# Flamingo layer on one core: list ends cleared by one queue two experts ahead, the first batch's q, k and maxima in another order, the last norms moved up

## What is computed

```
x = x + tanh(g_xattn) * attention(layernorm(x), ctx, ctx)      # 16 heads of 16
    energy = einsum('nqhd,nkhd->nhqk', qh, kh); attn = softmax(energy / 4); out @ Wo.T + bo
x = x + tanh(g_ffn) * ffn(layernorm(x))
    scores = softmax(xf @ w_router); top 2 of 8 experts
    h = silu(xf @ w1) * (xf @ w3); y = h @ w2                   # hidden 512, for each expert
    out = shared / 3 + moe_out * 2 / 3
```

## Time and profile before

| | us |
|---|---|
| median of 3 runs | 816.92 (815.06 to 818.07) |
| the profiled execution | 814.12 |
| its span, first to last instruction | 812.4 |
| PE busy in the span | 769.9 (95%) |
| DVE, POOL, ACT busy | 538.8, 430.7, 413.4 |
| mean granted clock of PE | 0.992 of full |

### The profile page before, as it was taken

How to read it: one execution, slowest core, us unless ns; L and a number is a source line. 1 busy time by engine, 2 the same in 40 slices (tenths; PEclk the granted TensorE clock), 3 DMA queues, 4 the chain that set the end, 5 groups by cost and what they waited for, 6 DMA issues and landing times.

```text
span 812.4 us, 19406 instructions
## 1 busy us (share of the span) xinstructions
PE 769.9 (95%) x6955; PEld 686.5 (85%) x6956; DVE 538.8 (66%) x1118; ACT 413.4 (51%) x690; POOL 430.7 (53%) x489
## 2 busy tenths in 40 slices
PE   4888999999999998898997999999999999999998
PEld 3756777777777776578997999999999999999998
DVE  5677889998888888857644444444444444446897
ACT  5667777777777767653324333333334334333332
POOL 5633446666666654457772476656756675236000
PEclk9999999999999999999998999999999999999999
DMA  6854557776666654244394354444543422317622
GB/s 213 272 179 158 173 185 231 234 235 209 210 209 209 198 182 145 93 170 138 110 248 113 96 155 130 117 114 131 142 116 78 111 70 58 72 53 306 233 93 79
DMA packets 129150, 127.34 MB, mean 157 GB/s; under 512 B 55232, under 2 KB 111040, under 8 KB 129088
## 3 DMA queue, kind: packets, MB, share of 16 engines
q1 hardware_dynamic: 114896, 80.34, 33.4%
q0 software_dynamic: 14192, 46.19, 16.9%
HBM read 75.32 MB, written 50.91 MB: 155 GB/s over the span
## 4 chain that ended last, share of the span: by engine, by line
PE 61%; POOL 10%; DMA 9%; issue 7%; DVE 7%; ACT 4%; SPq 2%; POOLq 1%; ACTq 0%; DVEq 0%
PE bank L562 7%; PE bank L563 6%; PE bank L564 6%; PE bank L643 6%; PE bank_ss L614 6%; PE bank_sm L627 4%; POOL w_l L1635 4%; DMA y_d<-y_s,y_rows 3%; PE bank_sm L562 3%; PE bank_ss L562 3%; PE bank_sm L563 3%; PE bank_sm L564 3%; PE bank_ss L564 3%; PE bank_ss L563 3%; PE bank L650 3%
## 5 line engine op out<-in xcount | busy, mean ns | idle before, releaser
L1248 DVE TENSOR_REDUCE row_max<-bank_sm 128x4 f32<-128x1024 f32 x124 | 151.5, 1222 | 37.8 <-PE bank_sm L627 36.2
L953 ACT ACTIVATE probs_T<-bank_ss 128x1024 f32<-128x1024 f32 x123 | 126.5, 1028 | 18.9 <-PE bank_ss L614 17.9
L1227 DVE TENSOR_TENSOR gT_l<-gg,gT_h 128x1024 fp32r<-128x1024 f32 x49 | 66.8, 1363 | 102.0 <-ACT gT_h L1084 100.1
L562 PE MATMUL bank_sm<-xg_h,w_h 128*128 128x256 f32 x400 | 114.3, 286 | 7.1 <-DVE xg_l L1227 7.1
L562 PE MATMUL bank_ss<-xg_h,w_h 128*128 128x256 f32 x400 | 113.2, 283 | 0.5 <-DVE gg L1434 0.5
L563 PE MATMUL bank_sm<-xg_h,w_l 128*128 128x256 f32 x400 | 113.6, 284 | 0.0
L564 PE MATMUL bank_sm<-xg_l,w_h 128*128 128x256 f32 x400 | 113.5, 284 | 0.0
L564 PE MATMUL bank_ss<-xg_l,w_h 128*128 128x256 f32 x400 | 112.9, 282 | 0.0
L563 PE MATMUL bank_ss<-xg_h,w_l 128*128 128x256 f32 x400 | 112.9, 282 | 0.0
L562 PE MATMUL bank<-w_h,gT_h 128*128 128x256 f32 x392 | 111.1, 284 | 1.5 <-DVE gT_l L1227 1.5
L563 PE MATMUL bank<-w_h,gT_l 128*128 128x256 f32 x392 | 110.9, 283 | 0.0
(11 more groups left out here) (204 smaller groups left out, 1945.6 us busy)
## 6 DMA issues: line engine op xcount, KB each, us to landing
qk_d<-qk_s SPq DMA_DIRECT2D x64, 256.0 KB, 2.8
w_raw<-wall POOLq DMA_DIRECT2D x27, 512.0 KB
k<-qk_d SPq DMA_DIRECT2D x48, 256.0 KB
q<-qk_d SPq DMA_DIRECT2D x48, 256.0 KB
xq<-xs_d SPq DMA_DIRECT2D x140, 64.0 KB
y_pairs<-y_d POOLq DMA_DIRECT2D x16, 512.0 KB, 9.7
x<-x SPq DMA_DIRECT2D x16, 256.0 KB, 4.7
c_s<-ctxT SPq DMA_DIRECT2D x16, 256.0 KB, 3.1
```

What stands on the lines that cost most here:

```text
L562: pe.matmul(out, ah, bh, start=first and k == 0, stop=False)
L953: act.activation(pT[:, 2 * (pv % 4):2 * (pv % 4) + 2, :].rearrange("p h t -> p (h t)"), exp_bank(V.b, pv)[:, :], ACT.Exp, scale=D ** -0.5) ...
L1227: return v.tensor_tensor(dst, ps, high.bitcast(F32), ALU.subtract)
L1248: v.tensor_reduce(mx[B.slot][:, :, :].rearrange("p t (r q) -> p r t q", r=2)[:, :, :, p], max_bank(B.b, p)[:, :].rearrange("p (r t k) -> p ...
```

## The change

- **Clears.** POOL clears nothing any more. SP clears expert 0's end as before, then those of experts 1 and 2; the ends of 3 to 7 are cleared in the now unrolled head of SP's loop, one after `load_rows(u)` of u = 1, 3, 5, 7, 9, each waited for two tiles later.
- **Start.** SP loads batch 0's q terms ahead of storing batch 1's k. POOL makes batch 0's q low part ahead of the second half of batch 1's norm. Batch 0's maxima are turned, copied and sent in two halves (`turn_first`, `first_max`, `first_rows`), the first after four of the eight head pairs; batch 0's exponentials wait for one half each. `keep_warm` is cut from 14 to 4, and the 4 + 4 later ones go; batch 1's first scores no longer wait for the last maxima of batch 0. bv x Wo is computed earlier, in another bank. One `clear_v` on DVE moves from between batch 0's and batch 1's maxima to the next round.
- **Last norms.** DVE: variance and norm of x14 ahead of x13's positions and slots. POOL: the weight split `cut(1, 0)` of the first third ahead of x14's root and of the second scatter of x12.

```diff
@@ sync
             def max_rows(C):
-                sp.wait_ge(mT_ok, C.n(1, 1))
+                sp.wait_ge(mT_ok, C.n(1, 2))
...
+            def first_rows(half):
+                sp.wait_ge(mT_ok, half + 1)
+                for par in range(2):
+                    row = ROWS * par + MROW
+                    sp.dma_start(q4[0][row:row + 1, HALF * half:HALF * half + HALF, :].bitcast(F32),
+                                 first_mT[half][par:2 * HALF:2, :].bitcast(F32)).then_inc((first_mrow, mrow)[half], 16)
...
             load_x(Batch(3))
+            terms_in(b0, 0)
             half_out(b1, 1)
-            terms_in(b0, 0)
             load_c(Batch(3))
+            terms_in(b1, 1)
             half_out(b1, 0)
-            terms_in(b1, 1)
             load_x(Batch(4))
             terms_in(b1, 0)
+            first_rows(0)
             half_out(b2, 1)
+            half_out(b2, 0)
+            first_rows(1)
             terms_in(b2, 1)
-            half_out(b2, 0)
-            max_rows(b0)
             terms_in(b2, 0)
...
             load_tile(0)
-            clear_behind(sp, (2, 4, 6), z_done)
+            clear_behind(sp, (1, 2), z_done)
...
-            sp.wait_ge(z_done, 16 * 3)
-            sp.wait_ge(z_pool, 16 * 4)
+            sp.wait_ge(z_done, 16 * 2)
...
-            with sp.Fori(1, last3) as u:
+            for u in range(1, 2 * NX - 5):
+                if u % 2 and u > 1:
+                    sp.wait_ge(z_done, 16 * ((u + 3) // 2))
+                load_routed(u + 3)
+                load_rows(u)
+                if u % 2 and (u + 5) // 2 < NX:
+                    clear_behind(sp, ((u + 5) // 2,), z_done)
+            sp.wait_ge(z_done, 16 * (NX - 1))
+            with sp.Fori(2 * NX - 5, last3) as u:
                 load_routed(u + 3)
                 load_rows(u)
@@ tensor
-                if pv == 0:
+                if pv == 0 and V.b == 0:
+                    pe.wait_ge(first_mrow, 32)
+                if pv == (0 if V.b else HALF):
                     pe.wait_ge(mrow, V.n(32, 32))
...
-                moved(pe, mx_ok, B.n(PAIRS, p - among_first(B, 1)))
+                moved(pe, mx_ok, B.n(PAIRS, p - (among_first(B, 1) or B.b == 1 and p == 0)))
+                if among_first(B, 1) and p == 1:
+                    pe.wait_ge(gbo_ok, 1)
...
+            def turn_first(half):
+                pe.wait_ge(mx_ok, HALF * half + HALF)
+                moved(pe, mT_ok, half)
...
                     if B and among_first(B, 1) and p == 0:
-                        keep_warm(SS[:, 0:512], 14)
-                    if B and B.b == 1 and p == 1:
                         keep_warm(SS[:, 0:512], 4)
+                    if B and among_first(B, 1) and p == HALF + 1:
+                        pe.wait_ge(xnTl_ok, A.n(1, 1))
+                        turn_first(0)
                     if B:
                         scores_to_max(B, p)
+                    if p == 0 and C and among_first(C, 1):
+                        turn_first(1)
...
-                if B and among_first(B, 1):
-                    pe.wait_ge(mx_ok, PAIRS - 1)
-                    keep_warm(SM[:, 0:512], 4)
-                    turn_max(B, None)
@@ vector
+            residual_variance(x14)
+            norm(x14)
             positions(x13, rk_tail)
-            residual_variance(x14)
             list_slots(x13)
             divide(x15)
-            norm(x14)
             x_low_shared(1, 1)
@@ gpsimd
+                    if A and among_first(A, 1):
+                        leave_low(0, qh_ok, ql_ok)
                     po.wait_ge(rstd1_ok, Eb.n(1, 1))
...
-            scatter(Batch(NB - 4), 1)
...
+            cut(1, 0, which=(0,))
             root(bmv2, rstd2, var2_ok, x14, rstd2_ok)
-            cut(1, 0, which=(0,))
+            scatter(Batch(NB - 4), 1)
...
-            po.wait_ge(ends_ok, 1)
-            po.wait_ge(sc_done[0], NB * 32)
-            po.wait_ge(sc_done[1], NB * 32)
-            clear_behind(po, (1, 3, 5, 7), z_pool)
             po.wait_ge(tab_ok, 1)
             cut(2, 1)
```

More of the change, by code:

```diff
@@ L46 @@
 PAIRS = H // 2
+HALF = PAIRS // 2
 LATE = 2
@@ L409, in max_rows @@
             def max_rows(C):
-                sp.wait_ge(mT_ok, C.n(1, 1))
+                sp.wait_ge(mT_ok, C.n(1, 2))
                 for par in range(2):
                     row = ROWS * par + MROW
-                    sp.dma_start(q4[C.slot][row:row + 1, :, :].bitcast(F32), mT[8 * par:8 * par + 8, :].bitcast(F32)).then_inc(mrow, 16)
+                    sp.dma_start(q4[C.slot][row:row + 1, :, :].bitcast(F32), mT[par:H:2, :].bitcast(F32)).then_inc(mrow, 16)
+            def first_rows(half):
[4 more added lines that the diff above has]
+                                 first_mT[half][par:2 * HALF:2, :].bitcast(F32)).then_inc((first_mrow, mrow)[half], 16)
             def one(i):
@@ L682, in turn_max @@
                 r.then_inc(mT_ps, 1)
+            def turn_first(half):
+                pe.wait_ge(mx_ok, HALF * half + HALF)
+                moved(pe, mT_ok, half)
+                for qc in range(TC):
+                    r = pe.transpose(T0[0:2 * HALF, qc * P:(qc + 1) * P], mx[0][:, qc, 2 * HALF * half:2 * HALF * (half + 1)], ident)
+                r.then_inc(mT_ps, 1)
             def turn_out(S):
@@ L809, in one @@
                             project_rows(T2, t, c_h[A.c_slot], c_l[A.c_slot], wt_h[:, 2], wt_l[:, 2], v_ps)
-                    if p == 7 and A and A.b == 1:
+                    if p == 7 and A and A.b == 0:
                         pe.wait_ge(few_in, 64)
@@ L813, in one @@
                         for k in range(EC):
-                            r = pe.matmul(T0[:, 0:E], bv_s[:, k, :], wt_raw[:, 3, k * E:(k + 1) * E], start=k == 0, stop=k == EC - 1)
+                            r = pe.matmul(SS[:, 512:512 + E], bv_s[:, k, :], wt_raw[:, 3, k * E:(k + 1) * E], start=k == 0, stop=k == EC - 1)
                         r.then_inc(bo_ps, 1)
@@ L966, in from_bank, with first_max @@
                 act.activation(dst[:, :, :], bnk[:, :].rearrange("p (c t) -> p c t", c=EC), ACT.Copy).then_inc(done, 1)
+            def first_max(half):
+                act.wait_ge(mT_ps, half + 1)
+                act.activation(first_mT[half], T0[0:2 * HALF, 0:L], ACT.Copy, scale=-1.0).then_inc(mT_ok, 1)
             def out_high(S):
@@ L1004, in before @@
                                        ACT.Copy).then_inc(vr_ok, 1)
-                    if p == 0 and C:
-                        act.wait_ge(mT_ps, C.n(1, 1))
+                    if p == 0 and C and among_first(C, 1):
+                        first_max(1)
+                    if p == 0 and C and not among_first(C, 1):
+                        act.wait_ge(mT_ps, C.n(1, 2))
+                        act.wait_ge(first_mrow, 32)
                         moved(act, mrow, C.n(32))
                         act.activation(mT[:, :], mT_p, ACT.Copy, scale=-1.0).then_inc(mT_ok, 1)
+                    if p == HALF + 1 and i == -1:
+                        first_max(0)
                     if p == 1:
@@ L1215, in out_bias @@
                 v.wait_ge(few_in, 64)
-                link(v.tensor_tensor(gbo[:, :], T0[:, 0:E], gbo[:, :], ALU.add))
+                link(v.tensor_tensor(gbo[:, :], SS[:, 512:512 + E], gbo[:, :], ALU.add))
                 v.tensor_scalar(gbo[:, :], gbo[:, :], gate[:, 0:1], None, ALU.mult).then_inc(gbo_ok, 1)
@@ L1246, in row_max @@
                 if p == 0:
-                    moved(v, mT_ps, B.n(1, 1 - R))
-                v.tensor_reduce(mx[B.slot][:, :, :].rearrange("p t (r q) -> p r t q", r=2)[:, :, :, p],
+                    moved(v, mT_ps, B.n(1, 2 - R))
+                v.tensor_reduce(mx[B.slot][:, :, :].rearrange("p t (q r) -> p r t q", r=2)[:, :, :, p],
                                 max_bank(B.b, p)[:, :].rearrange("p (r t k) -> p r t k", r=2, t=TC), AX, ALU.max).then_inc(mx_ok, 1)
@@ L1411, in one @@
                     out_bias()
-                if A and A.b == R - 1:
+                if A and A.b == R:
                     clear_v(R)
@@ L1716, in one @@
                     root(bmv2, rstd2, var2_ok, S2, rstd2_ok)
-                if A:
+                if A and not among_first(A, 1):
                     leave_low(0, qh_ok, ql_ok)
```

11 lines of the change are left out of this document (5 added, 6 removed).

## The result

The changed kernel takes 806.51 us (median of 4 executions, 805.07 to 808.12) beside 816.95 (815.06 to 818.07) for the one before: the ratio is 0.987, 95% interval 0.9846 to 0.9894, so 10.4 us or 1.3% faster. On the chip with number 9 the same pair later gave 805.36 and 812.64, ratio 0.9906 (0.9890 to 0.9922), 7.6 us. The number of the first chip is not on record. The experiments ran on chip 9, those of the second series on chip 5, always beside the kernel before on the same chip. The profiled execution took 808.12 us, with a span of 806.3.

What follows compares the result with a forecast made beforehand. PE was taken as the bound nearly everywhere, so only its waits and low-clock stretches could pay. Terms of 8.0, 1.7 and 3.0 us sum to 12.7, taking the median of 816.92 to 804.2 us, range 800.0 to 809.5.

Steps and rivals of the forecast that it cites:

- What bounds the kernel: PE bounds nearly everywhere; an edit pays only where PE stands still or runs at its lower clock.
- Term A: Routed part, tile 7: with POOL's clears gone its rows land before PE needs them; 8.0 us gained, bounds 6.1 and 8.0.
- q0's remainder: Traffic left on POOL's DMA queue while tile 7 loads, once POOL's clears are gone: about 1.1 MB.
- The loop's clears, priced at nothing: Five clears in SP's loop hide ahead of later tile loads: cost nothing; uncovered, up to 3.2 us each.
- Term B: Last norms: two PE waits of about 1 us go, one of 0.4 comes; 1.7 us gained, bounds 0 and 2.1.
- the split ends before the root can be wanted: Last norms: POOL's weight split takes 3.6 us and is done in time, so x14's norm starts at about 362.3.
- The forecast wait of 0.4 for `o_s`: Last norms: `divide(x15)`, taken as 1.5 us, now follows norm and positions, so PE gets its result some 0.4 us late.
- Term C: Start: first scores 2.0 us sooner, plus 1.0 us up to batch 0's exponentials; 3.0 us gained.
- PE would wait for `row_max` anyway: Start: the reason only part of the 4 keep-warm products of 1.19 us ahead of the turn was charged.
- The rival "the start gives nothing": Start: k's loads become last in q's place, or a further low-clock stretch eats the gain; 807.2 us, chance 0.20.
- the prediction's own signs of it: Start: a granted clock clearly under 0.91 from 30 to 48 us, or a low stretch twice as long.
- The lock: End of the shared tiles: POOL's split beside DVE's `gT_l` makes that about 2.7 us; 0.7 lost, total 804.9, chance 0.12.

Runs made afterwards that it cites:

- filler cut: The kernel before with only the keep-warm products cut (14 to 4, both groups of 4 gone, with one group's wait): 815.01 us, ratio 1.004.
- clears doubled: The changed kernel with each of the five clears in SP's loop followed by an equal-sized write to unused device memory: 809.06 us, ratio 0.9953.
- the fastest kernel: The changed kernel with batch 1's q stored early, keep-warm products put in again, and batch 4's context loaded ahead of batch 2's k and q: 802.57 us.

## Why the prediction came out as it did

The prediction gave 804.2 and a range of 800.0 to 809.5; 806.51 was measured. The time fell inside the range, 2.3 us above the forecast. The mechanism of the clears was right, that of the norms half right, the start gave nothing, and what was priced at nothing is close to having a price. The range's lower end is not what its terms give: 804.2 − 0.4 − 0.9 − 0.5 − 1.6 is 800.8, even with all of them at once.

- **What bounds the kernel**: right. The attention loop did not move (254.63 and 254.50 us of 264), and all gains and losses lie where PE waits or its clock is low.
- **Term A, 8.0 us**: mechanism right in every step: q0's remainder was forecast at 1.1 MB and is 1.19, tile 7 lands before it is needed, tile 8 comes 17.26 us after tile 6, and the two profiles differ there by 7.98. Its size was off. The term was read from one execution, in which the wait was 6.10 us and the low stretch behind it long. Three other profiles with the old clears (norms only, start only, filler cut) have waits of 2.9, 3.5 and 3.2, and from tile 6's to tile 8's high part 21.90, 22.50 and 22.25 us: 4.6, 5.2 and 5.0 lost, not 7.97. The timed value is 6.3 (4.7 to 7.9).
- **The loop's clears, priced at nothing**: as far as the medians tell, the first set costs little: the clears-only kernel loses 0.7 of its 9.38 after tile 8, the two profiles of clears and norms 0.15 and −0.06. But the cover is nearly used up: a second set costs 3.8 us, where the prediction let both loads and a clear fit into a tile. The cover was sought at the tile loads, and the loss comes at the scatter of results, which the prediction did not look at. That loss is not the clears' alone: with the clears of before, the start-only kernel lost 3.5 us at the same place (−1.60 to +1.93) and the one with the filler cut 3.76. How long ACT waits there mostly goes with the loss (5.05 to 5.60 us with under 0.4 lost, 6.75 with 2.0, 7.65 with 3.5), with one exception (4.97 with 0.96). The wait has two parts. With the start only and with the filler cut POOL issues the scatter about 2.5 us later after tile 8 than in the kernel before (74.9 and 72.4 us), behind its longer wait for `y_rows`, and ACT goes on 2.43 us after the issue, as before (2.49); with the clears doubled the issue is 1.3 us later and those 2.49 become 4.45. What makes POOL's wait long in one kernel and short in another is open.
- **Term B, 1.7 us**: 1.50 in the changed kernel, 1.7 in the three with the norms and without the start. The reason given was half right. The norm is fast (0.74), since POOL no longer splits beside it; but "the split ends before the root can be wanted" failed, the root is 2.1 us late, and both waits of PE go only because what is left fits. The forecast wait of 0.4 for `o_s` is there, 0.32, but its reason was misread: the row of `o_s` in the earlier trace rows gives 0.76 us for both halves together (362.82 to 363.58), and `divide(x15)` was put at 1.5.
- **Term C, 3.0 us**: the step that failed. First scores were forecast 2.0 sooner and it was 1.55. But batch 0's exponentials were to come 3 us sooner (43.7) and came 0.4 later (in a second profile of the changed kernel 0.59 sooner). Two things were overlooked. The keep-warm products were charged as an obstacle that could only go away ("PE would wait for `row_max` anyway"); they held the clock (0.84 without them, 0.94 with, over 20 to 48), and cutting them alone costs 3.2 us, where I had allowed 1.6. Where those 3.2 us are lost is not shown, as said above. And only batch 0's transfers were followed: q of batch 1 came behind the loads of its k. The rival "the start gives nothing", 807.2, describes the outcome best, and the prediction's own signs of it are there: 0.82 over 30 to 48, clearly under 0.91, and a low stretch of 41.6 to 48.4 where the longest at the start of before took 3.4 us. Alone the part loses 3.2 us, with the other two it is neutral; that these differ goes with the clock (0.987 against 0.993 alone, a loss of 0.006; 0.993 against 0.995 and 0.996 together, 0.002 to 0.003), but why the loss is smaller there was not settled.
- **The lock**: not at the forecast place. `gT_l` at 411.60 takes 1.21 us, not 2.7; POOL's cast, started 0.15 us after it, takes 1.96, not 1.06 as in the earlier trace rows. One tile on `gT_l` takes 2.25, in slack.
- **The sum** 12.7 became 10.4 in the first comparison and 7.6 on chip 9. From the parts timed alone on chip 9: 6.3 + 2.8 − 3.2 = 5.9. That the first comparison came within 2.3 us of the forecast is in part luck: terms A and C were both too large, and 816.92 less the 7.6 us of chip 9 would be 809.3, just inside the range.

## What to carry to other kernels

A stall that one profile shows is one sample: where it ends in a low-clock stretch, its length and that of the stretch differ by several us between executions, so take the term's size from several profiles. Before you cut filler products of an idle PE, time the kernel with only that edit, and look in its trace for where the time goes: a lower clock at the place of the edit need not be where it is lost. When a stall at the start is shortened, follow the next batch's transfers through the issuing queue as well: here each gain of 2 us was lost again within the same round, to the one load that had not moved, until that was moved too.

## What the runs showed of the hardware

The time of one and the same kernel goes with its granted clock: in the 23 executions of the kernel before in the first series, those at 0.996 took 809.6 us on average, at 0.994 811.3, at 0.992 813.0, and the one at 0.987 815.5. So much of what looks like noise between executions goes with how long PE ran at the lower level; longer waits and a lower clock come together, and these times do not separate them. In the changed kernel's profile it did so from 21.1 to 24.5, 41.6 to 48.4 and 51.8 to 55.2, the first two after PE had waited (2.20 us for `xn_s` ahead of 20.74, 3.70 for q ahead of 41.49); in the fastest kernel the stretch from 20 to 48 ran at full clock, although PE waited the same 2.2 us for `xn_s` there. The Trainium skill, page "TensorE: Matmul & The Clock Gate", section "HAM oscillation — how this bites in real kernels", describes a kernel in which every wait for a transfer lets the clock fall, so that the work behind it starts slow; the filler experiment agrees, 0.94 to 0.84 over 20 to 48. The fastest kernel shows that not every such wait does it.

The two-way lock: when POOL's cast and DVE's `gT_l` met at 411.6, the one issued second took the delay, 1.96 us for a cast of 1.06; at 418.47, where POOL had begun the first half of its split at 418.34, it was DVE, 2.25 for 1.21, and then the second half of the split, begun at 419.60, 2.28 for 1.28. The Trainium skill, page "SBUF — State Buffer", section "Who interferes with whom", says that issue order decides who blocks, not the kind of operation. These rows agree with that. A row of the kernel before is not explained by the start times of the two operations alone: `gT_l` at 400.56 took 2.73 us, though POOL's cast beside it began later, at 401.15, and took 1.06; POOL's scatter had begun at 400.18.
